# The two parts of h, q and the router's weight as scaled 16-bit floats in an attention and routed-expert kernel

## The reference, cut to what matters

```python
# x: 4 sequences of 1024 tokens, width 128, float32
x = x + attn(layernorm(x), w_lhs, w_rhs)
x = x + moe(layernorm(x), router_w, w_fc, b_fc, w_proj, b_proj)

def attn(h, w_lhs, w_rhs):                     # one head of width 128
    scores = einsum('nsd,ntd->nst', h * w_lhs, h * w_rhs)
    return einsum('nst,ntd->nsd', softmax(scores, axis=2), h)

def moe(x, ...):                               # 8 experts, hidden 512, the best 2 per token
    probs = softmax(x @ router_w.T)
    topk, idx = top_k(probs, 2);  topk /= topk.sum()
    # each chosen expert: gelu(x @ w_fc[e] + b_fc[e]) @ w_proj[e] + b_proj[e], times its weight
```

## Time and profile before

| | us |
|---|---|
| median of 3 runs | 310.75 (310.5 to 311.79) |
| profiled execution, span | 352.5 |
| PE busy | 281.2 (80% of the span) |
| PE weight loads | 247.1 (70%) |
| DVE busy | 230.5 (65%) |
| ACT busy | 197.3 (56%) |
| POOL busy | 178.5 (51%) |
| chain that ended last | PE 65%, DVE 12%, issue 10%, no known releaser 4%, ACT 3% |

### The profile page before, as it was taken

One profiled execution on the slowest core, in us unless ns is written; L12 is line 12 of the kernel. 1 busy time (PEld: TensorE's weight loads), 2 busy tenths in 40 slices (PEclk: granted clock), 3 DMA queues, 4 the chain that ended last, 5 costly groups with the idle time before them and its releaser, 6 DMA issues.

```text
span 352.5 us, 8201 instructions
## 1 busy us (share of the span) xinstructions
PE 281.2 (80%) x2223; PEld 247.1 (70%) x2223; DVE 230.5 (65%) x972; ACT 197.3 (56%) x427; POOL 178.5 (51%) x243
## 2 busy tenths in 40 slices
PE   7999999999949987799496353999969999978200
PEld 3689997989748975689486233999959989977200
DVE  4898988889636896887775224685545555634265
ACT  3363778873648634365694213577658888855100
POOL 8030260285757358585777575455554555444500
PEclk9999999999979999999999685899999999989855
DMA  6930000012110001014213221113222222210199
GB/s 214 420 145 0 3 0 3 0 38 87 55 40 32 2 23 48 31 48 126 68 48 108 70 71 53 47 40 94 74 73 80 70 62 79 65 37 32 37 376 338
DMA packets 15450, 28.51 MB, mean 81 GB/s; under 512 B 3904, under 2 KB 9920, under 8 KB 15152
## 3 DMA queue, kind: packets, MB, share of 16 engines
q1 hardware_dynamic: 10800, 17.93, 15.4%
q0 software_dynamic: 4608, 10.07, 8.6%
HBM read 15.83 MB, written 12.16 MB: 79 GB/s over the span
## 4 chain that ended last, share of the span: by engine, by line
PE 65%; DVE 12%; issue 10%; another core or an unknown queue 4%; ACT 3%; POOL 2%; DMA 2%; POOLq 0%; ACTq 0%; DVEq 0%; SPq 0%
PE av_ps L1319 19%; PE av_ps L1114 14%; PE sc_ps L1300 5%; PE sc_ps L1298 5%; PE sc_ps L1299 4%; DVE neg_piece L1435 4%; PE bank L1285 3%; PE sc_ps L1103 2%; DVE res L1823 2%; PE bank L1090 1%; PE bank L1099 1%; DVE res L1821 1%; PE bank L1092 1%; PE bank L1091 1%
## 5 line engine op out<-in xcount | busy, mean ns | idle before, releaser
L887 POOL DMA_INDIRECT results<-prob,result_row x71 | 68.2, 961 | 62.3 <-PE sc_ps L1300 26.6
L1319 PE MATMUL av_ps<-raw_proj,raw_fc 128*128 x568 | 78.1, 287 | 19.1 <-issue 16.0
L1319 PEld LDWEIGHTS av_ps<-raw_proj,raw_fc 128*128 128x128 f32 x568 | 70.9, 199 | 22.1 <-issue 21.7
L1031 ACT ACTIVATE raw_fc<-sc_ps,bfc,scale_down 128x256 f32<-128x256 f32 (+1 forms) x188 | 80.7, 516 | 3.7 <-remote 3.5
L783 POOL DMA_INDIRECT slots<-stage,slot x64 | 62.6, 978 | 30.4 <-issue 20.2
L1114 PE MATMUL av_ps<-h_all,prob 128*128 128x137 f32 x512 | 74.3, 288 | 0.1
L1114 PEld LDWEIGHTS av_ps<-h_all,prob 128*128 128x128 f32 x512 | 67.7, 192 | 4.2 <-DVE res L1463 1.4
L1777 DVE TENSOR_TENSOR h_all<-av_ps,bpr 128x256 f32<-128x256 f32 (+1 forms) x47 | 16.9, 360 | 63.5 <-remote 35.0
L1023 ACT ACTIVATE h_all<-bank 128x512 f16<-128x512 f16 (+1 forms) x47 | 23.0, 493 | 58.9 <-remote 36.1
L1298 PE MATMUL sc_ps<-h_all,wfc_hi 128*128 128x256 f16 (+1 forms) x188 | 44.2, 252 | 4.2 <-issue 2.9
L1300 PE MATMUL sc_ps<-h_all,wfc_lo 128*128 128x256 f16 (+1 forms) x188 | 44.1, 252 | 2.8 <-issue 2.8
(11 more groups left out here) (184 smaller groups left out, 516.7 us busy)
## 6 DMA issues: line engine op xcount, KB each, us to landing
slots_in<-slots SPq DMA_DIRECT2D x24, 132.0 KB
raw_fc<-in_w_fc_dram SPq DMA_DIRECT2D x1, 2048.0 KB, 11.3
raw_proj<-in_w_proj_dram SPq DMA_DIRECT2D x1, 2048.0 KB, 15.7
raw_fc<-results SPq DMA_DIRECT2D x4, 512.0 KB, 5.1
raw_proj<-results SPq DMA_DIRECT2D x4, 512.0 KB, 8.0
out_dram<-res SPq DMA_DIRECT2D x8, 256.0 KB, 6.1
res<-in_x_dram SPq DMA_DIRECT2D x3, 512.0 KB, 5.9
slots_in<-slots SPq DMA_DIRECT2D x23, 66.0 KB
```

Source lines behind the costliest of these rows:

```text
L887: pool.indirect_dma_start(out=results[:, :], out_offset=bass.IndirectOffsetOnAxis(ap=result_row[a][:, h:h + 1], axis=0), in_=gated[a][h], ...
L1031: ins = act.activation(hid[:, a % NH, c, 0:halves_of(k) * P], up_ps(k, c), ACT.Gelu_apprx_tanh, bias=bfc[:, e, c:c + 1], scale=scale_down[ ...
L1319: mm = pe.matmul(o, hid[:, a % NH, c, rows], wpr[:, e, c, :], start=(c == 0 and h == 0), stop=(c == HC - 1), skip_group_check=True)
```

## The change

The eight arrays of parts become F16, that is 16 bits wide. To use the range of F16, h is made 4096 times as large (`H_UP`; through LayerNorm's variance, at no extra instruction), the product of the two weights is scaled by a power of two found from its own maximum (`scale_w`), and the router's weight by one found from its maximum over all partitions (`scale_rw`, with a second `partition_all_reduce` on POOL). The exponential gets a scale, `score_down`, that takes the powers of two out of the scores again, and the gap between the two best logits gets `rw_down`. The high part of the router's weight moves on ACT from the head of the program to behind `high_parts(1)`, and its low part on DVE behind the second `row_max`.

```diff
+H_UP = 2.0 ** 12
+RW_UP = 2.0 ** 13
...
-        hT_hi = sb("hT_hi", [P, 2, S], F32R)
-        hT_lo = sb("hT_lo", [P, 2, S], F32R)
-        q_hi = sb("q_hi", [P, 2, S], F32R)
-        q_lo = sb("q_lo", [P, 2, S], F32R)
+        hT_hi = sb("hT_hi", [P, 2, S], F16)
+        hT_lo = sb("hT_lo", [P, 2, S], F16)
+        q_hi = sb("q_hi", [P, 2, S], F16)
+        q_lo = sb("q_lo", [P, 2, S], F16)
...
-        rw_parts = sb("rw_parts", [P, 2 * E], F32R)
+        rw_parts = sb("rw_parts", [P, 2 * E], F16)
...
             sp.dma_start(w_d[:, 1:2], w_rhs).then_inc(w_in, 16)
+            for i, w in enumerate((w_lhs, w_rhs)):
+                sp.dma_start(w_rows[:, i, :], w.rearrange("d o -> o d").to_broadcast([P, D])).then_inc(w_in, 16)
             sp.dma_start(rwT[:, :], router_wT).then_inc(rw_in, 16)
...
-            for u in range(4):
+            for u in range(2):
+                scale(u)
+            pool.wait_ge(rwpeak_made, 1)
+            pool.partition_all_reduce(rw_peaks[:, :], rw_peak[:, :], P, RMAX).then_inc(rwpeaks_made, 1)
+            for u in range(2, 4):
                 scale(u)
...
-                act.activation(probT[:, m % RING, :], exp_source(n), ACT.Exp).then_inc(exp_made, 1)
+                act.activation(probT[:, m % RING, :], exp_source(n), ACT.Exp, scale=score_down[:, 0:1]).then_inc(exp_made, 1)
...
-            act.wait_ge(rw_in, 16)
-            act.activation(rw_hi, rwT[:, :], ACT.Copy).then_inc(rwhi_made, 1)
             for t in range(TU):
                 normalise(0, t)
             act.wait_ge(w_made, 1)
             for u in range(2):
                 high_parts(u)
+            act.wait_ge(rwup_made, 1)
+            act.activation(rw_hi, rwT[:, :], ACT.Copy, scale=rw_up[:, 0:1]).then_inc(rwhi_made, 1)
...
+            def scale_w():
+
+                dve.wait_ge(w_in, 64)
+                dve.tensor_tensor(w_rows[:, 2, :], w_rows[:, 0, :], w_rows[:, 1, :], ALU.mult).then_inc(w_chain, 1)
+                dve.tensor_tensor(w_d[:, 2:3], w_d[:, 0:1], w_d[:, 1:2], ALU.mult).then_inc(w_chain, 1)
...
+                dve.tensor_scalar(w_d[:, 2:3], w_d[:, 2:3], w_up[:, 0:1], 0.5, ALU.mult, ALU.mult).then_inc(w_made, 1)
+
+            def scale_rw():
+
+                dve.wait_ge(rwpeaks_made, 1)
+                dve.tensor_scalar(rw_peaks[:, :], rw_peaks[:, :], 2.0 ** -100, 2.0 ** 126, ALU.max, ALU.min).then_inc(rw_chain, 1)
...
+                dve.tensor_scalar(rw_up[:, :], rw_up[:, :], RW_UP, None, ALU.mult).then_inc(rwup_made, 1)
...
-            dve.wait_ge(w_in, 32)
-            dve.tensor_tensor(w_d[:, 2:3], w_d[:, 0:1], w_d[:, 1:2], ALU.mult).then_inc(w_made, 1)
-            dve.wait_ge(rwhi_made, 1)
-            dve.tensor_tensor(rw_lo, rwT[:, :], rw_hi.bitcast(F32), ALU.subtract).then_inc(rwlo_made, 1)
+            dve.wait_ge(rw_in, 16)
+            dve.tensor_reduce(rw_peak[:, :], rwT[:, :], AX_X, ALU.max, apply_absolute_value=True).then_inc(rwpeak_made, 1)
+            scale_w()
...
                     if b == 0 or n >= 1:
                         row_max(b, n)
+                    if b == 0 and n == 0:
+                        scale_rw()
+                    if b == 0 and n == 1:
+                        low_rw()
```

More of the change, by code:

```diff
@@ L128, in preln_attention_moe @@
         w_d = sb("w_d", [P, 3], F32)
+        w_rows = sb("w_rows", [P, 3, D], F32)
+        w_peak = sb("w_peak", [P, 1], F32)
+        w_pow2 = sb("w_pow2", [P, 1], F32)
+        w_up = sb("w_up", [P, 1], F32)
+        score_down = sb("score_down", [P, 1], F32)
+        rw_peak = sb("rw_peak", [P, 1], F32)
+        rw_peaks = sb("rw_peaks", [P, 1], F32)
+        rw_pow2 = sb("rw_pow2", [P, 1], F32)
+        rw_up = sb("rw_up", [P, 1], F32)
+        rw_down = sb("rw_down", [P, 1], F32)
         ident = sb("ident", [P, P], F32)
@@ L286, in preln_attention_moe @@
         w_made = sem("w_made")
+        w_chain = sem("w_chain")
+        rwpeak_made = sem("rwpeak_made")
+        rwpeaks_made = sem("rwpeaks_made")
+        rw_chain = sem("rw_chain")
+        rwup_made = sem("rwup_made")
         rwhi_made = sem("rwhi_made")
@@ L712, in _ @@
             pool.memset(neg_cols[:, :, :], 0.0).then_inc(consts, 1)
-            pool.memset(h_aug[:, :, :, D:D + 1], 1.0).then_inc(consts, 1)
+            pool.memset(h_aug[:, :, :, D:D + 1], H_UP).then_inc(consts, 1)
             pool.wait_ge(consts, N_CONSTS - 3)
@@ L1370, in take_stats @@
                     dve.wait_ge(rstd_made, u - 3)
-                dve.tensor_scalar(var_eps[:, u % 4, :], moments[:, u % 2, :, 1], EPS, None, ALU.add).then_inc(var_made, 1)
+                dve.tensor_scalar(var_eps[:, u % 4, :], moments[:, u % 2, :, 1], EPS, H_UP ** -2, ALU.add, ALU.mult).then_inc(var_made, 1)
             def take_spread(u):
@@ L1385, in low_parts @@
                 src = bank[u % 2 if u < 2 else 0][:, :]
-                dve.tensor_tensor(hT_lo[:, b % 2, cols], src, hT_hi[:, b % 2, cols].bitcast(F32), ALU.subtract).then_inc(hTlo_made, 1)
-                dve.scalar_tensor_tensor(out=q_lo[:, b % 2, cols], in0=src, scalar=w_d[:, 2:3], in1=q_hi[:, b % 2, cols].bitcast(F32),
+                dve.tensor_tensor(hT_lo[:, b % 2, cols], src, hT_hi[:, b % 2, cols], ALU.subtract).then_inc(hTlo_made, 1)
+                dve.scalar_tensor_tensor(out=q_lo[:, b % 2, cols], in0=src, scalar=w_d[:, 2:3], in1=q_hi[:, b % 2, cols],
                                          op0=ALU.mult, op1=ALU.subtract).then_inc(qlo_made, 1)
@@ L1427, in find_scales @@
                 link(dve.tensor_scalar(scale_down[:, :], pow2[:, :], 1.0 / TOP, None, ALU.mult))
+            def scale_w():
+                dve.wait_ge(w_in, 64)
+                dve.tensor_tensor(w_rows[:, 2, :], w_rows[:, 0, :], w_rows[:, 1, :], ALU.mult).then_inc(w_chain, 1)
+                dve.tensor_tensor(w_d[:, 2:3], w_d[:, 0:1], w_d[:, 1:2], ALU.mult).then_inc(w_chain, 1)
+                dve.wait_ge(w_chain, 2)
+                dve.tensor_reduce(w_peak[:, :], w_rows[:, 2, :], AX_X, ALU.max, apply_absolute_value=True).then_inc(w_chain, 1)
+                dve.wait_ge(w_chain, 3)
+                dve.tensor_scalar(w_peak[:, :], w_peak[:, :], 2.0 ** -100, 2.0 ** 126, ALU.max, ALU.min).then_inc(w_chain, 1)
+                dve.wait_ge(w_chain, 4)
+                dve.tensor_scalar(w_pow2[:, :].bitcast(U32), w_peak[:, :].bitcast(U32), 0x7F800000, None, ALU.bitwise_and).then_inc(w_chain, 1)
+                dve.wait_ge(w_chain, 5)
+                dve.reciprocal(w_up[:, :], w_pow2[:, :]).then_inc(w_chain, 1)
+                dve.tensor_scalar(score_down[:, :], w_pow2[:, :], 2.0 * H_UP ** -2, None, ALU.mult).then_inc(w_chain, 1)
+                dve.wait_ge(w_chain, 7)
+                dve.tensor_scalar(w_d[:, 2:3], w_d[:, 2:3], w_up[:, 0:1], 0.5, ALU.mult, ALU.mult).then_inc(w_made, 1)
@@ L1429, in row_max, with low_rw @@
+            def low_rw():
+                dve.wait_ge(rwup_made, 1)
+                dve.wait_ge(rwhi_made, 1)
+                dve.scalar_tensor_tensor(out=rw_lo, in0=rwT[:, :], scalar=rw_up[:, 0:1], in1=rw_hi,
+                                         op0=ALU.mult, op1=ALU.subtract).then_inc(rwlo_made, 1)
             def row_max(b, n):
@@ L1558, in find_gap @@
                     dve.wait_ge(gate_exp, r)
-                dve.tensor_tensor(gap[:, mine], step_down[:, mine], rstd2[:, b % 2, mine], ALU.mult).then_inc(gap_made, 1)
+                dve.scalar_tensor_tensor(out=gap[:, mine], in0=step_down[:, mine], scalar=rw_down[:, 0:1], in1=rstd2[:, b % 2, mine],
+                                         op0=ALU.mult, op1=ALU.mult).then_inc(gap_made, 1)
             def keep_ranks(r):
```

6 lines of the change are left out of this document (added).

## The result

The changed kernel takes 312.74 us in the median of 6 runs (312.35 to 314.74), the kernel before 310.53 beside it (310.09 to 311.79). The ratio is 1.0075, 95% interval 1.0054 to 1.0096: slower by 2.2 us. The range of the forecast, 305.4 to 315.5, holds it; the forecast itself, 310.2 and no change that could be told, does not.

What follows compares the result with a forecast made beforehand. PE was taken to set the pace in mid-batch and DVE at the heads of batches and program. From 310.75 us, PE's saving of 3.0 and the head's loss of 2.5 gave 310.2, range 305.4 to 315.5.

Steps and rivals of the forecast that it cites:

- the sentence on the broadcasts: Head, DVE: late broadcasts show up to 1 us at first, but are covered by the wait for POOL's reduction.
- The head's loss: Head, DVE: waiting for POOL's new reduction moves the second maximum from 14.36 to 16.66; 2.5 us lost in all.
- The way to the reduction: Head, POOL: changing configuration before the new reduction takes 6.73 us, possibly 0 to 9.5.
- The way back: Head, POOL: changing configuration back takes another 6.7 us, covered because DVE's statistics come only at 23.5.
- PE's saving: Attention stage, PE: 16-bit matmuls save 3.0 us, 1.7 in mid-batch and 1.3 at batch heads; bounds 0 and 7.9.
- DVE's wait before the sixth maximum: Batch heads: DVE's waits for PE, 0.71 us in batch 1 and 0.58 in batch 2, bound the gain and disappear.
- a tile of the router's matmuls: Batch heads, PE: the router's two matmuls fall from 0.23 to 0.11 us, saving 0.12 a tile.
- the first matmul behind attention: Score blocks, PE: it costs 0.09 us more than in the stream; 16-bit weights take off 0.05.
- The other edits: Mainly ACT: the exponential's scale from memory costs 0.086 us each, counted as 0 in time, 5.5 us as bound.
- The slower one: Head, POOL: configuration code loads slowly while DMA is full, PE idles, its clock drops; 313.5 to 316.9 us, chance 0.26.
- The clock's fall in the first 25 us: Head, PE: a sign that, if seen in the changed kernel's profile, the forecast is wrong.
- 16 bits do nothing: Score stream: 16 bits gain nothing, or exponentials bind; the head's 2.5 us is lost, giving 313.3 us, chance 0.08.

Runs made afterwards that it cites:

- f5: The changed kernel with the weights' power of two as a constant and no broadcast loads, only the router's searched for: 313.92 us, ratio 1.0128.
- f1: The changed kernel plus five idle 16-bit matmuls in PE's wait for the experts' rows near 205 us: 313.65 us, ratio 1.0100.
- e3: The changed kernel with both powers of two as constants, no searches, the exponential's scale still read from memory: 308.40 us, ratio 0.9932.
- e2: The changed kernel with both powers of two as constants, no searches, the exponential's scale an immediate: 308.70 us, ratio 0.9941.
- second set: The changed kernel, unaltered, timed and profiled once more: 313.75 us, ratio 1.0108.
- g5: The kernel before plus the two broadcast loads behind the router's weight, with nobody waiting for them: 310.26 us, ratio 1.0014.
- e5: The kernel before plus the two broadcast loads ahead of the router's weight, with DVE waiting for them: 313.74 us, ratio 1.0103.
- h2: The change with both powers found by PE matmuls instead of broadcasts and POOL's reduction, DVE's order turned at batch 3's head: 308.56 us, ratio 0.9939.

## Why the prediction was wrong

**The step that failed** is the term at which the prediction put the two broadcasts, next to nothing, in the sentence on the broadcasts, "If the two new broadcasts land late, up to 1 us of that shows at first, but lies under the wait for the reduction." Its size was wrong: nine instructions start at 9.54, where I had them fit before 8.63, and h's second half starts at 11.15, 2.52 late, of which 0.91 are the landing and 1.61 the instructions that it uncovered. Their length was forecast well; that they lie in a wait was not. Its cover was wrong: the first row of the loss is PE's wait of 2.29 for h, which moves both the first and the second maximum, and the reduction was through before DVE asked.

**The head's loss** was forecast at 2.5 for the second maximum, with 16.66 as its start. It started at 16.50, 2.14 late. That agreement is an accident: the sum had POOL's reduction as its term, and in the profile DVE's wait for it is 0; the first maximum, which I had left in its place, is 2.07 late already, by the broadcasts and the instructions behind them. The second profile of the change, with 6.7 us for the same load and a fall of the clock, put the first score 2.63 later still.

**The way to the reduction** was taken as 6.73. It took 6.3 to 8.0 in seven profiles, and in the change it is hidden. By the Trainium skill, page "GPSIMD Engine Reference", section 2.1 (Instruction dispatch), it would be about 6, 5.95 as measured there, for the first call; the trace shows 6.3 at the least. The way back was taken as 6.73 too; POOL's next instruction came 9.42 us behind the reduction in f5, and 10.59 in f1, waiting for nothing known, and there it was not covered, as I had it.

**PE's saving** was forecast at 3.0; it is 1.6 in the time, and 2.3 in the profile with constants up to the experts. The distance of 0.216 held, and so did DVE's wait before the sixth maximum, gone in batches 1 and 2. Batch 0 gave 0.60 and batch 3 0.34 where I had 0.42, batch 1 1.33 where I had 1.13. The term that failed is batch 2, 0.06 in place of 1.0: I took DVE's wait of 0.58 there as what reaches the end, and POOL's twelve scatters were. Two sizes were smaller as well: a tile of the router's matmuls saves 0.085, not 0.12 (the two take 0.05 in place of 0.23, but the attention's pair between two tiles grew from 0.23 to 0.32), and the first matmul behind attention gives next to nothing, by the same trade (0.32 to 0.21, and the eight ahead of it 0.84 to 0.93).

**The other edits** held: exponentials at 0.688, forecast 0.685, and no cost in e3's median.

**The rivals.** The slower one named the right mechanism, PE idle at the head and then the lower clock, with the wrong cause. It came about by the broadcasts, and by POOL alone only in f5. The clock's fall in the first 25 us, which I had named as a sign that the forecast is wrong, is in the second profile of the change and not in the first. The rival's direction is what came out, at a price of 2.2 us over the kernel before, where I had 2.8 and more. "16 bits do nothing", at 313.3, is nearest in time and wrong in its terms: 16 bits gained, and the 2.5 lost was not POOL's.

So the account is: 16 bits -1.6 (e2) to -1.9 (e3), the search +4.0, or +5.0 by the second set. Of the search 2.1 us are the head of an execution without a fall of the clock there, and with the load later by another 0.7 to 0.8 us and a fall at the head they are 4.4 to 4.7. The sum is shown by the runs with constants, and what each fall costs by the profiles; in what part of the executions each comes, and so the split of the median, is not. That it is the waits that bring the falls about is borne out at the head: with the wait filled the clock stayed up in three profiles of three, unfilled it fell in four of five. For the other places it is argued.

## What to carry to other kernels

A small load is as late as what stands ahead of it in its queue: put the one that is waited for first (g5 against e5), and don't count a load's bytes but the time that rows like it took to land. Here the order alone would not have helped, since the broadcasts were waited for too. A chain that is hidden in a wait is hidden only as long as its inputs are there when the wait begins. A value that all partitions need can be spread by a matmul against the identity, in a wait that is there anyway, in place of a broadcast or a reduction on POOL. And a faster PE waits longer for the others; look where its idle times grow, because the clock may go with them.

## What the runs showed of the hardware

- Two loads of 64 KB, each one row of 512 bytes copied to 128 partitions, ran in a stretch of 33 to 54 GB/s with the DMA engines 0.17 to 0.23 busy (change), and landed after 4.5 to 7.0 us (nine profiles).
- The same load of 4 KB behind them took 5.8 to 6.7 us from execution to execution, and without them ahead 2.6 to 2.9, once 4.1 (h2).
- A change of POOL's configuration costs differently each time, 6.3 to 8.0 us on the way in and 6.7 to 10.6 on the way out.
- The same wait of PE, 2.13 to 2.14 us in the same place, was followed by the lower clock in four profiles of ten; one of 2.53 to 2.66 us near 171 in 12 of 16, where it cost nothing by the last scatter; the falls near 208 cost about 2 us.
- Matmuls of no use in PE's waits made the time 2.0 to 3.6 us longer than the span, in place of 1.7 to 2.0.
